# Wider first passes, context keys stacked on TensorE, and no idle matmuls in a two-attention decoder layer

## The chip, the cores and the metric

One core of one Trainium2 chip runs the whole program. The metric is the time on the device of one execution in microseconds (us). A core has five engines that run side by side and meet at semaphores: TensorE (PE in the profile, PEld for its weight loads), VectorE (DVE), ScalarE (ACT), GpSimd (POOL) and SyncE (SP), which here issues the DMA transfers.

## The reference

Two batches of 256 tokens with 128 features pass through three blocks, each followed by a residual sum and a layer norm. Block A is attention in which all 16 heads (8 features each) share one key and one value. Block X adds a causal self-attention (B below) and an attention over 512 context tokens (C below). The last block is a gated feed-forward over 8 experts, the best two weighted.

```python
q = (hidden_states @ Wq.T + bq) * SCALING        # block A: k and v are one head for all 16
scores = jnp.einsum('bthd,bsd->bhts', q, k)
probs = jax.nn.softmax(scores, axis=-1)
...
att = jnp.einsum('bhqd,bhkd->bhqk', q, k) * scale           # B, causal
y = jnp.einsum('bhqk,bhkd->bhqd', jax.nn.softmax(att, axis=-1), v)
attc = jnp.einsum('bhqd,bhkd->bhqk', qc, kc) * scale        # C, 512 context keys
y = y + jnp.einsum('bhqk,bhkd->bhqd', jax.nn.softmax(attc, axis=-1), vc)
...
for e in range(E):                                          # E = 8
    h = jnp.einsum('btd,hd->bth', x, W1[e]) + b1[e]
    a, b = jnp.split(h, 2, axis=-1)
    out = out + (jnp.einsum('bth,dh->btd', a * jax.nn.sigmoid(b), Wo) + bo) * comb[..., e:e + 1]
```

## The kernel before

Everything after the loads stays on the chip. Each engine works through its own list of jobs, written out by hand in the table `ORDER`. A token such as `SC0021:w0` is a job (kind SC, batch 0, query tile 0, pair 2, head 1 of the pair) and the PSUM buffer that it writes. An engine takes its jobs strictly in the order of the table, so a job that waits holds back all that stand behind it. A buffer is handed on by counters: `take` waits until its last reader has emptied it.

There are eight PSUM banks of 512 columns: three single buffers w0, w1 and w2, two double ones t0 and t1 (1024 columns), and y.

Scores are computed with bf16 operands at the accuracy of float32. A projection is split into three bf16 parts whose sum is the value (kinds h, d, f and g: ScalarE makes the high part, VectorE or GpSimd the two others), and the parts are stacked along the contraction rows, rows 0 to 47 for the even head of a pair of heads and 64 to 111 for the odd one, by matmuls with a matrix of zeros and ones (kinds R, line 380) and a copy (kinds e). The context keys are the exception: GpSimd makes their lower parts (`kc`, lines 1075 to 1080), and twelve DMAs (`K`, line 1181) put the parts in their rows.

Softmax takes two passes over the scores. The first (kinds S, lines 475, 491 to 494 and 502) computes them with queries on the partitions, and VectorE takes the largest of each row (kinds M, lines 796, 804 and 811), one buffer of 512 columns and one head at a time. The negated maxima are split into bf16 parts (kinds s), transposed by TensorE (kinds T, line 512) and copied (cT) to a row buffer; two DMAs for each group (kinds m, line 1171) write them into three more rows of the stacked queries. The second pass (kinds U, lines 522, 535 to 540 and 549) computes the transposed scores with the maximum already subtracted; ScalarE takes the exponential of 1024 columns (kinds E, line 979), and TensorE multiplies with the values (kinds P, lines 564, 582 and 599), where the row sum comes along as a ninth column. Kinds Y, n, Z, W, z, r, l and X transpose, normalise and project the result. Kinds F are the experts (lines 675 and 676).

The last digits of a job name batch, tile or group: UA10 is the second pass of block A, batch 1, pair 0. JQC0 (line 426) is the first projection of block X for batch 0. `N` (line 406) are matmuls on zeros whose result nobody reads.

## Time and profile before

| | us |
|---|---|
| median of 3 timed runs | 223.85 |
| lowest and highest | 222.95, 237.25 |
| the profiled execution, its own time | 221.34 |
| its span in the profile | 219.4 |

The span is what the trace covers, from the first to the last instruction. The execution's own time is 1.94 us longer. TensorE's clock as granted by the chip was 0.882 of full speed on average.

### The profile page before, as it was taken

How to read it: one execution, taken by the hardware profiler on the slowest of the kernel's cores; microseconds unless marked ns; L12 is line 12 of the kernel's file. 1: busy time of each engine (PE TensorE's matmuls, PEld its weight loads, DVE VectorE, ACT ScalarE, POOL GpSimd, SP SyncE). 2: the span in 40 equal slices, each digit the busy share in tenths (PEclk: the TensorE clock that was granted, in tenths of full speed). 3: DMA queues.
4: the chain of work that ended last, by engine and by line, in shares of the span. 5: the costliest groups of instructions: out<-in, count | busy, mean ns of one | idle time of the engine just before them, and what ended most of it. 6: DMA issues, size and time to landing. Idle time of an engine off the chain costs nothing.

```text
span 219.4 us, 4917 instructions
## 1 busy us (share of the span) xinstructions
PE 189.2 (86%) x1918; PEld 99.8 (45%) x1918; DVE 153.3 (70%) x390; ACT 103.0 (47%) x146; POOL 60.5 (28%) x171
## 2 busy tenths in 40 slices
PE   6979798840089999999989999999999999999981
PEld 3437243420024442455556545756576554445440
DVE  7983895850006857899789689793772589888883
ACT  3452075310057752446639866763957632242230
POOL 2199679431000010111440030020121316403204
PEclk9975558985559855899999999999999999999999
DMA  6960003555400000000000000000000000000001
GB/s 141 352 242 0 7 2 56 66 62 63 50 0 0 0 3 1 3 5 4 0 6 4 0 3 4 4 0 6 3 6 3 0 1 0 4 0 0 12 0 37
DMA packets 3910, 6.34 MB, mean 29 GB/s; under 512 B 880, under 2 KB 1640, under 8 KB 3888
## 3 DMA queue, kind: packets, MB, share of 16 engines
q1 hardware_dynamic: 3888, 6.03, 12.5%
q8 instruction: 15, 0.25, 0.5%
q14 instruction: 7, 0.06, 0.1%
HBM read 4.02 MB, written 0.26 MB: 20 GB/s over the span
## 4 chain that ended last, share of the span: by engine, by line
PE 67%; DVE 15%; DMA 9%; ACT 4%; issue 3%; POOLq 0%; POOL 0%; DVEq 0%; SPq 0%; ACTq 0%
PE t L675 9%; DMA q_stack_A<-mrow_A 8%; PE w L502 6%; PE y L599 6%; PE t L380 4%; PE t L549 4%; PE y L564 4%; PE w L491 3%; DVE mneg L811 3%; PE w L494 3%; PE w L475 3%; PE t L522 2%; PE t L676 2%; DVE mneg L796 2%; PE t L540 2%
## 5 line engine op out<-in xcount | busy, mean ns | idle before, releaser
L979 ACT ACTIVATE probs<-t 128x1024 f32<-128x1024 f32 x60 | 58.4, 1025 | 45.2 <-PE t L522 26.0
L811 DVE TENSOR_REDUCE mneg<-w 128x1 f32<-128x512 f32 x64 | 41.5, 685 | 7.3 <-PE w L502 6.8
L675 PE MATMUL t<-w1T,x1T 128*128 128x512 f32 x64 | 33.3, 601 | 0.2 <-DVE val_c L904 0.2
L796 DVE TENSOR_REDUCE mneg<-w 128x2 f32<-128x512 f32 x32 | 20.4, 686 | 4.9 <-PE w L475 4.5
L522 PE MATMUL t<-q_stack_A,k_stack_a 51*128 51x256 bf16 x64 | 9.4, 353 | 15.3 <-DMA q_stack_A<-mrow_A 14.5
L502 PE MATMUL w<-k_stack_c,q_stack_C 48*128 48x512 bf16 x64 | 21.7, 415 | 0.5
L1105 POOL CAST mpart<-mneg 128x8 bf16<-128x8 f32 (+1 forms) x11 | 2.1, 194 | 72.0 <-DVE mneg L811 48.9
L1018 ACT ACTIVATE part_c<-t 128x512 f32<-128x512 f32 x16 | 9.6, 597 | 26.1 <-PE t L676 24.0
L804 DVE TENSOR_REDUCE mneg<-w 128x2 f32<-128x512 f32 (+1 forms) x24 | 16.2, 686 | 7.7 <-PE w L494 7.6
L599 PE MATMUL y<-probs,v_c 128*32 128x128 f32 x512 | 17.2, 276 | 0.0
L475 PE MATMUL w<-k_stack_a,q_stack_A 48*128 48x256 bf16 x64 | 13.3, 344 | 2.7 <-DVE mneg L796 2.7
L675 PEld LDWEIGHTS t<-w1T,x1T 128*128 128x128 f32 x64 | 11.3, 190 | 8.3 <-issue 5.8
L599 PEld LDWEIGHTS y<-probs,v_c 128*32 128x32 f32 x512 | 13.0, 109 | 3.0 <-issue 1.9
L522 PEld LDWEIGHTS t<-q_stack_A,k_stack_a 51*128 51x128 bf16 x64 | 3.5, 108 | 20.7 <-DMA q_stack_A<-mrow_A 14.7
L549 PE MATMUL t<-q_stack_C,k_stack_c 51*128 51x128 bf16 x256 | 12.7, 218 | 0.2
L676 PE MATMUL t<-b_stack,bias_sel 128*128 128x512 bf16 x32 | 12.1, 379 | 0.0
L984 ACT ACTIVATE y_sb<-y 128x512 f32<-128x512 f32 x12 | 7.1, 595 | 10.3 <-PE y L564 5.3
L845 DVE COPY x1T<-w 128x256 f32<-128x256 f32 x2 | 0.8, 420 | 15.5 <-PE w L651 15.5
L920 DVE SCALAR_TENSOR_TENSOR ctx_room<-val_c,gate_comb,ctx_room 128x256 f32<-128x256 f32 x20 | 9.9, 494 | 1.7 <-DVE val_c L904 0.5
L549 PEld LDWEIGHTS t<-q_stack_C,k_stack_c 51*128 51x128 bf16 x256 | 7.7, 94 | 6.2 <-ACT probs L979 2.3
L564 PE MATMUL y<-probs,v_a 128*32 128x512 f32 x64 | 10.5, 749 | 0.0
L491 PE MATMUL w<-k_stack_b,q_stack_B 48*128 48x128 bf16 (+1 forms) x64 | 10.3, 270 | 0.0
(207 smaller groups left out, 316.6 us busy)
## 6 DMA issues: line engine op xcount, KB each, us to landing
w1T<-in_w1T SPq DMA_DIRECT2D x8, 256.0 KB, 6.7
k_stack_c<-part_c SPq DMA_DIRECT2D x12, 128.0 KB
rest<-in_rest SPq DMA_DIRECT2D x1, 772.0 KB, 7.5
bias_row<-in_rows SPq DMA_DIRECT2D x1, 384.0 KB, 6.1
ctx_room<-in_ctx SPq DMA_DIRECT2D x1, 320.0 KB, 5.3
first<-in_first SPq DMA_DIRECT2D x1, 262.5 KB, 2.8
q_stack_C<-mrow_C SPq DMA_DIRECT2D x16, 3.0 KB
out<-rest SPq DMA_DIRECT2D x4, 64.0 KB, 1.5
```

The costliest lines, as they stand in the source:

```text
L475: last = nc.tensor.matmul(o[:, a * T:(a + 1) * T], q_stack["A"][half(i), p, q0 + a * P:q0 + (a + 1) * P], k_stack_a[half(i), b, :], start= ...
L491: nc.tensor.matmul(o[:, m * keys:(m + 1) * keys], q_stack["B"][half(i), p, q0 + q * P:q0 + (q + 1) * P], k_stack_b[half(i), p, q0:q0 + key ...
L502: give(nc.tensor.matmul(o[:], q_stack["C"][half(i), p, q0 + q * P:q0 + (q + 1) * P], k_stack_c[half(i), p, b * TC:(b + 1) * TC], start=Tru ...
L522: last = nc.tensor.matmul(o[:, c0:c0 + T], k_stack_a[half(i, KROW), b, kt * P:(kt + 1) * P], q_stack["A"][half(i, KROW), p, q0:q0 + T], st ...
L549: last = nc.tensor.matmul(o[:, c0:c0 + P], k_stack_c[half(i, KROW), p, b * TC + kt * P:b * TC + (kt + 1) * P], q_stack["C"][half(i, KROW), ...
L564: last = nc.tensor.matmul(y_open[32 * j:32 * j + VW, :], v_a[:, 2 * b + kt, :], moving, start=(kt == 0), stop=(kt == 1), tile_position=(0, ...
L599: last = nc.tensor.matmul(y_open[32 * j:32 * j + VW, c * P:(c + 1) * P], v_c[:, 4 * b + kt, VD * head:VD * head + VW], probs[:, u, c0:c0 + P],
L675: nc.tensor.matmul(o, x2T[:, (2 * b + q) * P:(2 * b + q + 1) * P], w1T[:, e, :], start=True, stop=False)
L676: last = nc.tensor.matmul(o, bias_sel[:, e, :], b1_stack[:], start=False, stop=True)
L796: emptied(V.tensor_reduce(out=mneg[:, mb_of[("A", b, p // 4)], at:at + 9:8], in_=o[:].rearrange("p (a k) -> p a k", a=2), axis=AX.X, op=AL ...
L811: emptied(V.tensor_reduce(out=mneg[:, mb_of[("C", b, q, p // 4)], at:at + 1], in_=o[:], axis=AX.X, op=ALU.max, negate=True), src)
L979: emptied(A.activation(probs[:, n % NPT, :], o[:], ACT.Exp), src)
```

## The change

The PSUM banks are divided anew: one single buffer w0, three double ones t0, t1 and t2, and y.

A first-pass job now computes the scores of both heads of a pair into one double buffer, and one VectorE instruction reduces 1024 columns. Its matmuls alternate between the two halves of the contraction rows.

The lower bf16 parts of the queries and keys of block A and of the context keys are made on TensorE and ScalarE: a new job D repeats the projection and subtracts the parts that are already there by a matmul with the negated unit matrix, and ScalarE copies the remainder. For block X, VectorE subtracts, ScalarE makes the middle part and VectorE the last. The context keys are stacked like the others (RKC, eKC), so the twelve DMAs, GpSimd's parts and its eight fills of the key array go. The two R jobs of a projection run as one block of 24 matmuls over four groups of 32 rows. The factor of the scores moves into the exponential. All 12 idle matmuls go. The whole table `ORDER` is written anew; the diff shows a line of it.

```diff
--- before.py
+++ after.py
...
-        N3:w0 JQA0:w0 JQA1:w1 JKA0:w2 JKA1:w0 RQA00:t0 RQA01:t1 RKA0:w2 KC:t0 SA030:w1 SA031:w2 SA001:w0 SA011:w1 SA020:w0
...
+        JKA0:w0 VA:t0 JQA0:t1 DKA01 DQA01 DKA02 DQA02 RKA0:w0 JKA1:t2 RQA00:t1 JQA1:w0 RQA01:t0 DQA11 DKA11 SA02:t1 SA01:t0
...
-        w0 w1 w2 w3 w4 w5 w6 w7 mA00 mA01 K00 K10 K02 K12 K01 K11 K03 K13 K05 K15 K04 K14 bb mA10 mA11 mC000 mB00 mC001 mC010
-        mB01 mC011 mC100 mC101 mB10 mC110 mC111 mB11 st01 st10 st00 st11""",
+        w0 w1 w2 w3 w4 w5 w6 w7 mA00 bb mA01 mA10 mA11 mC001 mC000 mB00 mB01 mC010 mC011 mC100 mC101 mB10 mC110 mB11 mC111 st00
...
-        region = {"w0": ps("w0", [P, 512]), "w1": ps("w1", [P, 512]), "w2": ps("w2", [P, 512]),
-                  "t0": ps("t0", [P, 1024]), "t1": ps("t1", [P, 1024]), "y": ps("y", [P, 512])}
+        region = {"t0": ps("t0", [P, 1024]), "t1": ps("t1", [P, 1024]), "t2": ps("t2", [P, 1024]),
+                  "w0": ps("w0", [P, 512]), "y": ps("y", [P, 512])}
...
+                elif kind in ("DQA", "DKA", "DKC"):
+                    name, src, cols, count = split_of(kind, b)
+                    if once("ident_neg"):
+                        pe.wait_ge(s_ident_neg, 1)
+                    pe.wait_ge(s_parts[f"{name}{b}"], job[2])
+                    o = region[filled[src][0]][:, 0:count]
+                    if kind == "DKC":
+                        nc.tensor.matmul(o, wc[:, 0, :], ctxT[:, cols], start=True, stop=False)
+                    else:
+                        i = 0 if kind == "DQA" else 1
+                        nc.tensor.matmul(o, w_a[:, i * C:(i + 1) * C], x0T[b], start=True, stop=False)
+                    for r in range(job[2]):
+                        last = nc.tensor.matmul(o, ident_neg[:], parts_of[name][:, r, cols], start=False, stop=(r == job[2] - 1))
+                    last.then_inc(s_left[f"{name}{b}"], 1)
...
+                elif kind in ("RQA", "RQB", "RKB", "RQC", "RKC"):
+                    if once("sel"):
+                        pe.wait_ge(s_sel, 1)
+                    halves.append(take(slot, job))
+                    if job[2]:
+                        name = "qk"[kind[1] == "K"] + kind[2]
+                        side = 0 if kind[1] == "Q" else 1
+                        if kind[2] == "B" or kind == "RQC":
+                            pe.wait_ge(s_parts[f"{name}{b}"], 3)
+                        else:
+                            wait_emptied(pe, ("KC", b // 2) if kind == "RKC" else ("J" + kind[1:], b))
+                        values = parts_of[name][:, :, q0:q0 + T]
+                        lasts = {}
                         for j in range(2):
                             for r in range(3):
                                 for i in range(2):
-                                    c0 = i * 512 + j * T
-                                    last = select(o, slice(c0, c0 + T), side, j, r, 2 * job[2] + i, values[:, r, :])
-                    give(last, job)
+                                    for g in range(2):
+                                        c0 = i * 512 + j * T
+                                        lasts[g] = select(halves[g], slice(c0, c0 + T), side, j, r, 2 * g + i, values[:, r, :])
+                        for g in range(2):
+                            give(lasts[g], (kind, b, g))
+                        halves.clear()
...
                 elif kind == "SA":
-                    _, b, p, i = job
+                    _, b, p = job
                     if once(("kA", b)):
                         wait_emptied(pe, ("RKA", b))
                     if once(("qA", b, p // 4)):
                         wait_emptied(pe, ("RQA", b, p // 4))
                     o = take(slot, job)
                     for a in range(QT):
-                        last = nc.tensor.matmul(o[:, a * T:(a + 1) * T], q_stack["A"][half(i), p, q0 + a * P:q0 + (a + 1) * P],
-                                                k_stack_a[half(i), b, :], start=True, stop=True)
+                        for i in range(2):
+                            c0 = i * 512 + a * T
+                            last = nc.tensor.matmul(o[:, c0:c0 + T], q_stack["A"][half(i), p, q0 + a * P:q0 + (a + 1) * P],
+                                                    k_stack_a[half(i), b, :], start=True, stop=True)
...
                 elif kind == "SC":
-                    _, b, q, p, i = job
-                    if once("kC"):
-                        pe.wait_ge(s_kc, 16 * 12)
+                    _, b, q, p = job
+                    for n in (2 * b, 2 * b + 1):
+                        if once(("kC", n, p // 4)):
+                            wait_emptied(pe, ("RKC", n, p // 4))
                     if once(("qC", b, p // 4)):
                         wait_emptied(pe, ("RQC", b, p // 4))
                     o = take(slot, job)
-                    give(nc.tensor.matmul(o[:], q_stack["C"][half(i), p, q0 + q * P:q0 + (q + 1) * P],
-                                          k_stack_c[half(i), p, b * TC:(b + 1) * TC], start=True, stop=True), job)
+                    for i in range(2):
+                        last = nc.tensor.matmul(o[:, i * 512:(i + 1) * 512], q_stack["C"][half(i), p, q0 + q * P:q0 + (q + 1) * P],
+                                                k_stack_c[half(i), p, b * TC:(b + 1) * TC], start=True, stop=True)
+                    give(last, job)
...
                 elif kind == "MC":
-                    _, b, q, p, i = job
-                    src = ("SC",) + job[1:]
-                    at = 4 * i + p % 4
-                    o = wait_full(dve, src)
-                    emptied(V.tensor_reduce(out=mneg[:, mb_of[("C", b, q, p // 4)], at:at + 1], in_=o[:], axis=AX.X, op=ALU.max,
-                                            negate=True), src)
+                    _, b, q, p = job
+                    o = wait_full(dve, ("SC", b, q, p))
+                    dst = mneg[:, mb_of[("C", b, q, p // 4)], p % 4:p % 4 + 5:4]
+                    emptied(V.tensor_reduce(out=dst, in_=o[:].rearrange("p (i k) -> p i k", i=2), axis=AX.X, op=ALU.max,
+                                            negate=True), ("SC", b, q, p))
...
+                if kind in ("hQA", "hKA", "hQB", "hKB", "hQC", "hKC"):
+                    name, src, cols, count = split_of(kind, b)
+                    if name in left and job[2]:
+                        wait_emptied(act, src)
+                    else:
+                        o = wait_full(act, src)
+                        if job[2]:
+                            act.wait_ge(s_left[f"{name}{b}"], job[2])
+                    dst = parts_of[name][:, job[2], cols]
+                    value = left[name][:] if job[2] and name in left else o[:, 0:count]
                     if name in PROJ_BIAS:
-                        ins = A.activation(parts_of[name][:, 0, cols], o[:, 0:T], ACT.Identity,
-                                           bias=bias_col[:, PROJ_BIAS[name]:PROJ_BIAS[name] + 1], scale=PROJ_SCALE[name])
+                        ins = A.activation(dst, value, ACT.Identity, bias=bias_col[:, PROJ_BIAS[name]:PROJ_BIAS[name] + 1])
                     else:
-                        ins = A.activation(parts_of[name][:, 0, cols], o[:, 0:T], ACT.Copy)
-                    ins.then_inc(s_parts[f"{name}{b}"], 1)
-                elif kind in ("fQB", "fKB", "fQC"):
-                    name = "qk"[kind[1] == "K"] + kind[2]
-                    src = ("J" + kind[1:], b)
-                    o = wait_full(act, src)
-                    ins = A.activation(left[name][:, cols], o[:, 0:T], ACT.Identity,
-                                       bias=bias_col[:, PROJ_BIAS[name]:PROJ_BIAS[name] + 1], scale=PROJ_SCALE[name])
-                    if kind == "fQC":
-                        ins.then_inc(s_val[name], 1)
+                        ins = A.activation(dst, value, ACT.Copy)
+                    if job[2] < 2:
+                        ins.then_inc(s_parts[f"{name}{b}"], 1)
                     else:
                         emptied(ins, src)
...
-                    emptied(A.activation(probs[:, n % NPT, :], o[:], ACT.Exp), src)
+                    emptied(A.activation(probs[:, n % NPT, :], o[:], ACT.Exp, scale=SCALE), src)
...
-                elif kind == "kc":
-                    if b == 0:
-                        wait_emptied(pool, ("KC",))
-                    cols = slice(b * T, (b + 1) * T)
-                    link(G.tensor_tensor(val_c[:, cols], val_c[:, cols], part_c[:, 0, cols], ALU.subtract))
-                    link(G.tensor_copy(part_c[:, 1, cols], val_c[:, cols]))
-                    G.tensor_tensor(part_c[:, 2, cols], val_c[:, cols], part_c[:, 1, cols], ALU.subtract).then_inc(s_kc_parts, 1)
...
-                elif kind == "K":
-                    _, i, t = job
-                    if (i, t) == (0, 0):
-                        sp.wait_ge(s_ones_c, 1)
-                        sp.wait_ge(s_kc_high, 1)
-                    if (i, t) == (0, 1):
-                        sp.wait_ge(s_kc_parts, 4)
-                    row = HALF * i + D * t
-                    sp.dma_start(k_stack_c[row:row + D, :, :], part_c[half(i, HALF), TERM_PART_K[t], :]).then_inc(s_kc, 16)
...
```

How the change moves instructions, at three places. In these lists w and t stand for the PSUM buffers, `still` for the zeros.

SyncE's queue, from the first transfer of row maxima of block A on; before, and then after. `b_stack` is the stacked expert bias.

```order
L1171 DMA q_stack_A<-mrow_A 3x4x256 x4
L1181 DMA k_stack_c<-part_c 8x8x1024 x12
L1188 DMA b_stack<-gT 8x512 x2
L1188 DMA b_stack<-b_low 8x512
L1171 DMA q_stack_A<-mrow_A 3x4x256 x4
```

```order
L1155 DMA q_stack_A<-mrow_A 3x4x256 x2
L1163 DMA b_stack<-gT 8x512 x2
L1163 DMA b_stack<-b_low 8x512
L1155 DMA q_stack_A<-mrow_A 3x4x256 x6
L1155 DMA q_stack_C<-mrow_C 3x4x128 x4
```

The maxima of batch 1 stood behind the twelve key transfers and now follow those of batch 0 directly.

TensorE in block A, batch 0, up to the first transposed maxima (L512 before, L538 after) and the first second pass (L522, L548).

```order
L380 MATMUL w<-part_k,sel 128x256 x3
L464 MATMUL w<-ctx_room 128x128 x4
L416 MATMUL w<-first 128x8 x4
L475 MATMUL w<-k_stack_a,q_stack_A 128x256 x2
L512 MATMUL w<-ident_bf,mpart 24x128 x2
L475 MATMUL w<-k_stack_a,q_stack_A 128x256 x12
L522 MATMUL t<-q_stack_A,k_stack_a 128x256 x4
```

```order
L433 MATMUL w<-ctx_room 128x512
L438 MATMUL w<-part_c,ident_neg 128x512
L538 MATMUL t<-ident_bf,mpart 24x128 x2
L494 MATMUL t<-k_stack_a,q_stack_A 128x256 x4
L433 MATMUL w<-ctx_room 128x512
L438 MATMUL w<-part_c,ident_neg 128x512 x2
L373 MATMUL t<-part_q,sel 128x256 x24
L494 MATMUL t<-k_stack_a,q_stack_A 128x256 x4
L481 MATMUL w<-ctx_room 128x128 x4
L548 MATMUL t<-q_stack_A,k_stack_a 128x256 x8
```

The values (L416) and the context values (L464) leave the place ahead of the transposes; the remainders of the context keys (L433, L438), a stacking block and the context values now stand between the transposes and the second pass.

TensorE in block X: first passes over the context for batch 1 (L502, L527) among second passes (L549, L575) and value products (L599, L625) of batch 0.

```order
L502 MATMUL w<-k_stack_c,q_stack_C 128x512 x3
L599 MATMUL y<-probs,v_c 32x128 x16
L549 MATMUL t<-q_stack_C,k_stack_c 128x128 x8
L502 MATMUL w<-k_stack_c,q_stack_C 128x512 x2
L549 MATMUL t<-q_stack_C,k_stack_c 128x128 x8
```

```order
L527 MATMUL t<-k_stack_c,q_stack_C 128x512 x4
L575 MATMUL t<-q_stack_C,k_stack_c 128x128 x8
L625 MATMUL y<-probs,v_c 32x128 x16
L575 MATMUL t<-q_stack_C,k_stack_c 128x128 x8
L527 MATMUL t<-k_stack_c,q_stack_C 128x512 x4
```

First passes come in blocks of two pairs, in the same buffers as the second passes.

## Rows read from the trace of the kernel before

**Rows 1.** The page, part 1: busy us, share of the span, instructions.

```profile
span 219.4 us, 4917 instructions
PE 189.2 (86%) x1918; PEld 99.8 (45%) x1918; DVE 153.3 (70%) x390; ACT 103.0 (47%) x146; POOL 60.5 (28%) x171
```

**Rows 2.** The page, part 4: the chain that ended last, shares by engine.

```profile
PE 67%; DVE 15%; DMA 9%; ACT 4%; issue 3%; POOLq 0%; POOL 0%; DVEq 0%; SPq 0%; ACTq 0%
```

**Rows 3.** The chain in order of time, 43 to 66 us: start, us, what.

```profile
44.18 16.88 DMA q_stack_A<-mrow_A
...
65.65 0.45 PE w L426
```

**Rows 4.** The timeline, 22 to 62 us: start, us, engine, line, what.

```profile
22.98 1.62 SPq L1171 DMA_DIRECT2D q_stack_A<-mrow_A  x2
...
26.32 0.37 PE L522 MATMUL t<-q_stack_A,k_stack_a 51*128 51x256 bf16 x1
...
33.29 7.89 SPq L1181 DMA_DIRECT2D k_stack_c<-part_c  x12
...
43.37 5.14 SPq L1171 DMA_DIRECT2D q_stack_A<-mrow_A  x4
...
61.11 1.03 PE L522 MATMUL t<-q_stack_A,k_stack_a 51*128 51x256 bf16 x8 [14.48 <-DMA q_stack_A<-mrow_A]
```

**Rows 5.** Stretches: PE, PEld, DVE, ACT, POOL busy (instructions), PEclk, DMA, GB/s.

```profile
3.50:65.60 62.10, 42.28 (x263) 21.02 (x263) 34.08 (x91) 20.60 (x28) 29.45 (x76) 0.70 0.40 85
65.60:94.70 29.10, 28.81 (x223) 12.29 (x223) 21.67 (x40) 16.85 (x22) 1.86 (x10) 0.77 0.01 2
94.70:170.10 75.40, 73.05 (x1228) 44.58 (x1228) 56.97 (x129) 49.59 (x62) 14.01 (x42) 1.00 0.01 3
170.10:213.20 43.10, 42.28 (x200) 20.84 (x199) 35.27 (x102) 14.06 (x33) 11.45 (x28) 1.00 0.01 2
```

**Rows 6.** Stretches cut where the granted clock changes, same columns.

```profile
0.00:3.50 3.50, 1.46 (x3) 0.28 (x3) 2.50 (x21) 1.49 (x2) 1.38 (x10) 1.00 0.47 123
...
14.50:34.70 20.20, 18.72 (x101) 9.29 (x101) 13.50 (x26) 6.40 (x7) 16.55 (x49) 0.50 0.02 4
34.70:48.60 13.90, 9.94 (x83) 5.21 (x79) 10.16 (x27) 5.99 (x9) 7.38 (x19) 0.98 0.55 69
...
75.70:89.10 13.40, 13.36 (x70) 4.59 (x66) 9.09 (x15) 4.60 (x6) 0.79 (x4) 0.50 0.01 2
```

**Rows 7.** The timeline of TensorE, 131 to 135 us, at full clock.

```profile
131.85 1.38 PE L380 MATMUL t<-part_k,sel 32*128 32x256 bf16 x24
...
134.57 0.40 PE L549 MATMUL t<-q_stack_C,k_stack_c 51*128 51x128 bf16 x8
134.81 0.59 PE L502 MATMUL w<-k_stack_c,q_stack_C 48*128 48x512 bf16 x2
135.33 1.08 PE L599 MATMUL y<-probs,v_c 128*32 128x128 f32 x32
```

**Rows 8.** The timeline of TensorE among the experts, at full clock.

```profile
192.94 1.02 PE L675 MATMUL t<-w1T,x1T 128*128 128x512 f32 x2
193.80 0.38 PE L676 MATMUL t<-b_stack,bias_sel 128*128 128x512 bf16 x1
194.01 0.27 PE L657 MATMUL w<-ident,x 128*128 128x128 f32 x1
```

**Rows 9.** The timeline of VectorE and ScalarE: reductions in a row, copies of 1024 columns.

```profile
131.67 3.20 DVE L811 TENSOR_REDUCE mneg<-w 128x1 f32<-128x512 f32 x5 [0.19 <-PE w L502]
...
138.24 1.27 DVE L790 TENSOR_SCALAR k_stack_b<-t,row_ones 128x1024 bf16<-128x1024 f32 x1
...
132.72 1.11 ACT L966 ACTIVATE k_stack_b<-t,row_ones 128x1024 bf16<-128x1024 f32 x1 [0.38 <-PE t L380]
```

**Rows 10.** The timeline around the first group of maxima, 17 to 22 us.

```profile
17.51 0.66 POOL L1078 TENSOR_TENSOR val_c<-val_c,part_c 128x256 f32<-128x256 f32 x1
...
19.33 0.20 POOL L1105 CAST mpart<-mneg 128x16 bf16<-128x16 f32 x1
```

More of the change, by code:

```diff
@@ L25 @@
 NEG = -1.0e30
-ONES = 1.0019378662109375
 HALF = 64
@@ new lines @@
+        RKC01:t1 YA00:w0 YA01:t2 UA10:t0 ZA0:w0 UA11:t2 UA12:t1 WA0:w0 UA13:t0 SA15:t2 RKC20:t1 RKC21:t2 XA0:w0 PA100 TA11:t0
+        JQC0:w0 JKB0:t1 JQB0:t0 PA101 JV0:w0 RQC00:t0 RQC01:t1 UA14:t2 SC005:t1 UA15:t0 SC001:t2 SC006:t1 SC003:t0 UA16:t2
+        UA17:t0 SC004:t2 SC007:t1 RQB00:t0 PA110 RQB01:t2 PA111 SC002:t1 SC000:t2 TC001:w0 YA11:w0 RKB00:t1 RKB01:t0 SC011:t2
+        YA10:w0 SB001:t0 TC000:t2 SB000:t1 ZA1:w0 SB011:t2 SB012:t0 SB013:t1 WA1:w0 SB010:t2 UC000:t1 UC001:t2 UC002:t1 TB00:w0
@@ L327, in stacked @@
                 return k_stack_a[:, b, :]
-            dst = k_stack_b if job[0] == "RKB" else q_stack[job[0][2]]
+            dst = {"RKB": k_stack_b, "RKC": k_stack_c}.get(job[0], q_stack[job[0][2]])
             return dst[:, 4 * job[2]:4 * job[2] + 4, b * T:(b + 1) * T]
@@ L431, in _ @@
-                    give(last, job)
-                elif kind in ("RQA", "RKA", "RQB", "RKB", "RQC"):
+                            last = nc.tensor.matmul(o[:, i * C:(i + 1) * C], x1T[:, q0 + i * P:q0 + (i + 1) * P], wx[:, 3, :],
+                                                    start=True, stop=True)
+                    else:
+                        i = ("JQB", "JKB", "JQC").index(kind)
+                        last = nc.tensor.matmul(o[:, 0:T], wx[:, i, :], x1T[:, q0:q0 + T], start=True, stop=True)
@@ L453, in _ @@
                     o = take(slot, job)
-                    for i in range(2):
-                        last = nc.tensor.matmul(o[:, i * 512:(i + 1) * 512], wc[:, 0, :],
-                                                ctxT[:, i * 512:(i + 1) * 512], start=True, stop=True)
-                    give(last, job)
+                    give(nc.tensor.matmul(o[:, 0:TC], wc[:, 0, :], ctxT[:, b * TC:(b + 1) * TC], start=True, stop=True), job)
                 elif kind == "VC":
```

262 lines of the change are left out of this document (106 added, 156 removed).

## The prediction

> **What bounds the kernel now.** I read the page first: TensorE is busy for 189.2 of 219.4 us, VectorE for 153.3 and ScalarE for 103.0 [rows 1], and the chain that ended last lies on TensorE for 67%, on VectorE for 15% and on DMA for 9% [rows 2]. So TensorE's work counts first, and one transfer stands out. The chain in order of time shows it: 16.88 us from 44.18 us on for two rows of maxima of a few KB, and the first projection of block X (JQC0) starts only at 65.65 us [rows 3]. The timeline tells why. The same kind of transfer for batch 0 is issued at 22.98 us, and the second pass that needs it starts at 26.32 us, 3.3 us later. For batch 1 the issue is at 43.37 us and the start at 61.11 us. Between the two stand the twelve key transfers, issued from 33.29 us on [rows 4], and the DMA engines are 0.55 busy from 34.7 to 48.6 us [rows 6].
>
> I cut the span at JQC0, and at 94.7, 170.1 and 213.2 us [rows 5]. Stretch one (3.5 to 65.6 us) has TensorE busy for 42.3 of 62.1 us at a mean clock of 0.70. In the other three it is busy for 144.1 of 147.6 us, VectorE for 113.9 (77%), ScalarE for 80.5. What is cheaper on TensorE there should show, as long as VectorE can follow. After 213.2 us come 6.2 us of closing steps that the change leaves alone, but for idle matmuls beside them.
>
> **Prices at full clock.** Of TensorE I take the distance from start to start, since a record's length holds a tail. Two records of a float32 matmul of 512 columns take 0.86 us and a bf16 one of 512 columns 0.21 us [rows 8]; with half the columns I take half, 0.43 and 0.11 (estimates). Eight second-pass matmuls of 128 columns take 0.24 us [rows 7], although in a row they would need 0.43 at the bf16 price: neighbours in opposite halves of the rows run together. Two first-pass matmuls of 512 columns plus what lies between take 0.52 us before the value product starts [rows 7]; 0.43 of it is their columns. 24 stacking matmuls over two row groups take 1.38 us [rows 7], about 1.3 without the tail.
>
> **The change part by part.**
>
> *The key transfers go.* Batch 1's maxima then need about 3.3 us from issue to use as batch 0's did: start at 46.7 instead of 61.1 us, **-14.4**. Next late is TensorE's own order: XA0 and JQC0 stand behind UA10 to UA13 and came 4.5 us after UA10 (65.65 against 61.11). JQC0 at 51.3 us, if nothing else in stretch one changed.
>
> *Work that TensorE gains in stretch one*, at full clock: remainders D for block A, 4 x (0.43+0.11) + 4 x (0.43+0.21) = 4.7; for the context keys, 2 x (0.86+0.21) + 2 x (0.86+0.43) = 4.7; four stacking blocks RKC between 0.7 (four row groups at once, half of 1.3) and 1.3, near the middle as weight loads bind, 4 x 1.0 = 4.0; PA100 moves ahead of JQC0, 1.0. It loses 8 idle matmuls (1.7) and, since both heads run together, 16 x (0.43 - 0.27) = 2.6. Net **+10.1 at full clock**. The clock sets the price: before it was at its lower level, 1.2 GHz, from 14.5 to 34.7 us, and at 2.4 GHz around that [rows 6]. D, float32 over all rows, is denser than what stood there; I take a mean of 0.85, so 11.9 us, with ends 10.1 and 20.2. Beside it lies the idle time of TensorE outside the DMA wait, 62.1 - 42.3 - 14.5 = 5.3 us. Also gone is a wait on GpSimd, whose key parts (from 17.51 us) held the first split of maxima back to 19.33 us: 1.8 [rows 10]; the split is on VectorE now. Stretch one: 51.3 + 11.9 - 5.3 - 1.8 = **56.1 us**. If all additions hid, 49.5; with the low clock throughout, 64.4.
>
> The D jobs put two round trips between TensorE and ScalarE ahead of the first scores, in place of VectorE's steps. No row shows such a trip; it lies between nothing (queries and keys alternate, so each hides the other's) and some 1 us each, a D of 0.54 to 0.64 and half of a copy that takes 1.11 for four times the columns [rows 9]. I take nothing, as TensorE is the busier one; the 2 us stay in the range.
>
> *ScalarE and VectorE in stretch one.* Evictions of stacked keys: 5 x 1.11 on ScalarE and 3 x 1.27 on VectorE [rows 9]; six key parts of 512 columns, at half the copy's price some 0.6 each (an estimate). ScalarE is busy for 20.6 of 62.1 us there [rows 5], so it covers them. VectorE loses the lower parts of block A and gets 16 reductions instead of 32.
>
> *First passes from JQC0 on.* 64 context matmuls in 32 pairs: 32 x (0.43 - 0.24) = 6.1. Causal ones: four pairs of tile 0 and eight of tile 1 save 0.21 each, 2.5. Six pairs of stacking blocks, 1.3 to 1.0 each: 1.8. Four idle matmuls 0.9, and PA100's 1.0. Together **-12.3**. Five reductions in a row take 3.20 us, so 0.63 each start to start [rows 9]; 512 columns at VectorE's pace are nearly all of it, so a double one should take 1.15 to 1.25, the price of the copy of 1024 columns (1.27) being an upper bound. 44 of them instead of 88 save VectorE 0 to 5 us, and two more evictions take 2.5. VectorE's 113.9 us stay within 3 us. In 135 us that is 84%, so it will bind more often, with all double buffers shared: I give **+2** back, between 0 and 12.3. These stretches: 147.6 - 12.3 + 2 = **137.3 us**, 130 to 148.
>
> **The sum.** 56.1 + 137.3 + 6.2 = 199.6 us of span, plus the 1.9 around it: **201.5 us**, I say 201, against the profiled execution's 221.34. The timed median was 2.5 above that; the other runs scatter by more, and I add nothing. About 2% is what a measurement of this kernel can tell from no change.
>
> **A rule on the clock.** The trace shows the clock at 2.4 GHz from the start, even before the first idle matmul at 1.2 us [rows 6], and at 1.2 GHz from 14.5 us on. The Trainium skill, page "TensorE: Matmul & The Clock Gate", Part 1, says that the throttled state is the default and that activity releases it; by it the start without idle matmuls would be slow. The first rows disagree with that default here. By the rule the first 3 us of work on TensorE would take 6, 204 us in all; by the rows nothing is added. It speaks for rival one and leaves the sum alone.
>
> **The rivals.**
>
> *One, the clock stays low in stretch one.* For it: from 14.5 to 34.7 us TensorE is busy for 18.7 of 20.2 us and still at 1.2 GHz [rows 6], so being busy does not raise it, and three of the idle matmuls stood at the very start. Against: from 94.7 us on, where float32 products recur all the time, it stays at 2.4 GHz [rows 5], and D is float32. Price: 20.2 instead of 11.9, so JQC0 at 64.4 us; **210 us**. Chance 0.16.
>
> *Two, the readers bind after JQC0.* S and U share three double buffers. Each holds one for its fill, 1.0 to 1.2 us of reading and two hand-overs, some 1.75 us; 100 such uses (44 first passes, 44 second, 12 stackings) are 175 us over three buffers, 58 us of some 100. That speaks against it on average, VectorE's 84% for it. All 12.3 us come back: **212 us**. Chance 0.14. The Trainium skill, page "TensorEngine Tiling (Array Packing)", PSUM Bottleneck, says that tiling speeds up TensorE but not the emptying of PSUM, which is this rival; by it the sum loses the 12.3.
>
> *Three, the change does not do what it says:* the transfer of maxima was late for another reason than the queue behind the keys. The DMA share of 0.55 while the keys' transfers are under way speaks against it [rows 6]. JQC0 would come 14.4 later, **216 us**. Chance 0.03.
>
> *Four, slower.* w0 is now the only small buffer; 45 jobs after JQC0 use it (projections, transposes), where three stood. TensorE's order is strict, so a job that waits for w0 stops all scores behind it. A hand-over is about 0.8 us by estimate, a fill of 0.2 and half of a 1024-column copy; most w0 jobs have others between them. It decides from 0.5 us of stop per use: 22.4 / 45. At 0.65 the time is **231 us**. Chance 0.03.
>
> *Five, better:* all additions of stretch one hide, and VectorE's 5 us count as well: 49.5 + 130.3 + 6.2 + 1.9, **188 us**. Chance 0.07.
>
> **How the numbers follow.** The forecast itself, 190 to 208, has 0.57. The range 187 to 214 holds it, rivals one and two and half of five. Faster by over 2% (below 219.4) has 0.95, within 2% 0.03, slower 0.02.
>
> **What would show it.** UA10 within 4 us of its transfer's issue and no PE wait on DMA over 3 us; JQC0 at 50 to 62 us; the clock in 5 to 50 us above 0.7; reductions of 1024 columns near 1.2 us; two context first-pass matmuls 0.24 us apart from the next work; VectorE 80 to 86% busy from JQC0 to the end. The prediction is wrong if TensorE shows waits on w0 or t buffers of over 10 us in all, or if stretch one ends after 65 us.

## The result, and the profile after

The changed kernel takes **205.2 us** (four runs, 203.09 to 207.77) where the kernel before takes 223.85 (the median of its compared runs, 222.95 to 225.05). The ratio is **0.913, 95% interval 0.902 to 0.924**. The profiled execution took 207.77 us, for a span of 206.0. Some executions of a program run longer at a lower granted clock (the mean clock of TensorE over the span); they are left out of every ratio and of what is called a compared run, and the one profiled here, at 0.914 against 0.936 and 0.937 of the others, is one of them.

The page of after, part 1 (busy us, share, instructions) and the chain that ended last, by engine:

```profile
PE 180.4 (88%) x2044; PEld 97.3 (47%) x2044; DVE 148.1 (72%) x326; ACT 115.8 (56%) x171; POOL 44.0 (21%) x136
...
PE 72%; DVE 13%; ACT 9%; issue 3%; DMA 1%; POOLq 0%; POOL 0%; DVEq 0%; ACTq 0%
```

Against [rows 1] TensorE is busy 9 us less, ScalarE 13 more, and DMA, 9% of the chain in [rows 2], has fallen to 1%. The stretches to JQC0 and from there to the 6.2 us of closing steps, as in [rows 5] (PE, PEld, DVE, ACT, POOL busy; granted clock; DMA share; GB/s), of after:

```profile
3.50:57.66 54.16, 48.12 (x405) 24.78 (x405) 33.60 (x73) 31.98 (x45) 17.10 (x48) 0.91 0.22 69
57.66:199.80 142.14, 130.92 (x1635) 71.62 (x1634) 109.18 (x225) 81.92 (x123) 22.80 (x70) 0.93 0.01 3
```

and of before, the last three stretches of [rows 5] taken as one:

```profile
65.65:213.20 147.55, 144.14 (x1645) 77.68 (x1646) 113.91 (x270) 80.45 (x116) 27.33 (x79) 0.95 0.01 3
```

JQC0 comes 8.0 us earlier, and what follows is 5.4 us shorter. In the second stretch TensorE is busy 13.2 us less, but idle for 11.2 us instead of 3.4. The wait for the maxima is gone. [Rows 4] shows it before; this is the same place in the timeline of after, SyncE's issue first and TensorE below:

```profile
45.19 1.44 SPq L1155 DMA_DIRECT2D q_stack_A<-mrow_A  x2
...
49.13 0.39 PE L548 MATMUL t<-q_stack_A,k_stack_a 51*128 51x256 bf16 x4 [0.28 <-ACT k_stack_c L975]
```

UA10 starts 3.9 us after the issue and waits 0.28 us for the buffer that ScalarE still reads (`k_stack_c`, line 975), not for DMA. The start of the program is new too:

```profile
7.19 1.06 PE L436 MATMUL w<-first 128*128 128x256 f32 x2
8.04 0.42 PE L438 MATMUL w<-part_k,ident_neg 128*128 128x256 bf16 x1
...
10.29 0.60 PE L436 MATMUL t<-first 128*128 128x256 f32 x2
10.72 0.38 PE L438 MATMUL t<-part_q,ident_neg 128*128 128x256 bf16 x2
```

Two float32 records of the same shape take 0.85 us from start to start at 7.19 us and 0.43 us at 10.29, though the clock column reads 1.00 for both. So the work of the first microseconds runs at half speed, and the column does not show it. The trace of the kernel before has the same slow start behind its three idle matmuls:

```profile
3.54 3.82 PE L411 MATMUL w<-first 128*128 128x256 f32 x8 [0.87 <-DMA first<-in_first]
```

The next job starts at 7.29 us, so these eight float32 records take 3.75 us, 0.94 for two where 0.43 is full speed. The first scores start at 14.95 us in after (10.27 before). The costliest groups (busy us, mean ns, idle before, releaser) of after:

```profile
L984 ACT ACTIVATE probs<-t 128x1024 f32<-128x1024 f32 x60 | 58.9, 1025 | 18.3 <-PE t L575 14.5
L821 DVE TENSOR_REDUCE mneg<-t 128x2 f32<-128x1024 f32 x32 | 37.7, 1218 | 9.2 <-PE t L527 9.1
...
L808 DVE TENSOR_REDUCE mneg<-t 128x4 f32<-128x1024 f32 x16 | 18.8, 1216 | 8.5 <-PE t L494 8.4
```

### The profile page after: what moved, and what is told of

The parts are those of the page before. It is cut to its first block, busy times and chain, and to the rows that moved or that the text cites. A ratio compares the mean times of both kernels' runs of the same rounds, so it can differ in the third digit from the quotient of the medians.

```text
span 206.0 us, 5104 instructions
## 1 busy us (share of the span) xinstructions
PE 180.4 (88%) x2044; PEld 97.3 (47%) x2044; DVE 148.1 (72%) x326; ACT 115.8 (56%) x171; POOL 44.0 (21%) x136
## 4 chain that ended last, share of the span: by engine, by line
PE 72%; DVE 13%; ACT 9%; issue 3%; DMA 1%; POOLq 0%; POOL 0%; DVEq 0%; ACTq 0%
PE t L701 14%; PE y L625 9%; ACT probs L984 5%; PE t L373 5%; PE t L575 4%; PE y L590 4%; DVE mneg L821 3%; PE t L702 3%; PE t L527 3%; DVE mneg L808 3%; PE y L608 3%; DVE mneg L815 2%; PE t L566 2%; PE t L561 2%; PE w L433 2%
## 5 line engine op out<-in xcount | busy, mean ns | idle before, releaser
L984 ACT ACTIVATE probs<-t 128x1024 f32<-128x1024 f32 x60 | 58.9, 1025 | 18.3 <-PE t L575 14.5
L821 DVE TENSOR_REDUCE mneg<-t 128x2 f32<-128x1024 f32 x32 | 37.7, 1218 | 9.2 <-PE t L527 9.1
L808 DVE TENSOR_REDUCE mneg<-t 128x4 f32<-128x1024 f32 x16 | 18.8, 1216 | 8.5 <-PE t L494 8.4
L625 PE MATMUL y<-probs,v_c 128*32 128x128 f32 x512 | 19.1, 294 | 0.0
L527 PE MATMUL t<-k_stack_c,q_stack_C 48*128 48x512 bf16 x64 | 13.4, 455 | 2.6 <-ACT q_stack_C L977 1.0
L625 PEld LDWEIGHTS y<-probs,v_c 128*32 128x32 f32 x512 | 14.2, 117 | 3.0 <-issue 1.4
L575 PE MATMUL t<-q_stack_C,k_stack_c 51*128 51x128 bf16 x256 | 12.5, 229 | 3.4 <-DVE mneg L815 1.1
L815 DVE TENSOR_REDUCE mneg<-t 128x4 f32<-128x1024 f32 (+1 forms) x12 | 14.0, 1215 | 1.7 <-PE t L516 1.7
L701 PEld LDWEIGHTS t<-w1T,x1T 128*128 128x128 f32 x64 | 11.2, 191 | 8.0 <-issue 5.9
L575 PEld LDWEIGHTS t<-q_stack_C,k_stack_c 51*128 51x128 bf16 x256 | 8.1, 99 | 10.3 <-issue 4.9
L930 DVE SCALAR_TENSOR_TENSOR ctx_room<-gated,gate_comb,ctx_room 128x256 f32<-128x256 f32 x18 | 8.8, 489 | 1.0
L914 DVE SCALAR_TENSOR_TENSOR gated<-part_c,t 128x512 f32<-128x512 f32 x11 | 7.5, 684 | 2.3 <-ACT part_c L1023 1.9
L963 ACT ACTIVATE part_c<-w,first 128x512 bf16<-128x512 f32 x6 | 4.1, 687 | 7.9 <-PE w L438 6.3
L494 PE MATMUL t<-k_stack_a,q_stack_A 48*128 48x256 bf16 x64 | 6.9, 289 | 1.4 <-DVE mneg L808 0.8
L548 PE MATMUL t<-q_stack_A,k_stack_a 51*128 51x256 bf16 x64 | 7.0, 294 | 1.0 <-DVE mneg L821 0.6
L527 PEld LDWEIGHTS t<-k_stack_c,q_stack_C 48*128 48x128 bf16 x64 | 3.1, 97 | 9.4 <-issue 3.5
```

What stands on the lines that cost most here:

```text
L527: last = nc.tensor.matmul(o[:, i * 512:(i + 1) * 512], q_stack["C"][half(i), p, q0 + q * P:q0 + (q + 1) * P], k_stack_c[half(i), p, b * TC ...
L575: last = nc.tensor.matmul(o[:, c0:c0 + P], k_stack_c[half(i, KROW), p, b * TC + kt * P:b * TC + (kt + 1) * P], q_stack["C"][half(i, KROW), ...
L625: last = nc.tensor.matmul(y_open[32 * j:32 * j + VW, c * P:(c + 1) * P], v_c[:, 4 * b + kt, VD * head:VD * head + VW], probs[:, u, c0:c0 + P],
L701: nc.tensor.matmul(o, x2T[:, (2 * b + q) * P:(2 * b + q + 1) * P], w1T[:, e, :], start=True, stop=False)
L808: emptied(V.tensor_reduce(out=dst, in_=o[:].rearrange("p (i a k) -> p i a k", i=2, a=2), axis=AX.X, op=ALU.max, negate=True), ("SA", b, p))
L815: emptied(V.tensor_reduce(out=dst, in_=o[:].rearrange("p (i m k) -> p i m k", i=2, m=count), axis=AX.X, op=ALU.max, negate=True), ("SB", b ...
```

## The experiments

### The maxima ahead of the keys

In the kernel before, SyncE's order alone:

```diff
-w7 mA00 mA01 K00 K10 ... K04 K14 bb mA10 mA11 mC000
+w7 mA00 mA01 mA10 mA11 K00 K10 ... K04 K14 bb mC000
```

> The kernel before, with only SyncE's order changed: the two transfers of batch 1's maxima stand ahead of the twelve key transfers and the bias transfers. Theory (the maxima were late because they stood behind the keys in one queue): UA10 starts within 4 us of its transfer's issue, at about 47 us instead of 61.1, JQC0 at about 51. The keys are now issued from about 44 us on and, at the 15 us that they took before from first issue to the end of the traffic, land at about 59 us, so the first context scores may wait for them some 4 us. Time 207 to 214 us, ratio 0.93 to 0.955. Rival (they were late for another reason): UA10 stays after 57 us, ratio within 2% of 1.

Its two compared runs took 227.8 and 227.9 us, before 223.8 in the same sitting and 222.7 to 223.7 in the next: no gain, 4 us lost. Timeline of SyncE, then of TensorE, in this run:

```profile
42.85 5.69 SPq L1171 DMA_DIRECT2D q_stack_A<-mrow_A  x4
48.66 7.94 SPq L1181 DMA_DIRECT2D k_stack_c<-part_c  x12
...
46.59 0.61 PE L522 MATMUL t<-q_stack_A,k_stack_a 51*128 51x256 bf16 x8
...
50.74 0.93 PE L426 MATMUL w<-x1T,rest 128*128 128x256 f32 x2 [0.28 <-DVE x1T L845]
...
75.56 0.60 PE L502 MATMUL w<-k_stack_c,q_stack_C 48*128 48x512 bf16 x1 [17.39 <-DMA k_stack_c<-part_c]
```

The first half of the theory holds: UA10 at 46.59 us, JQC0 at 50.74, as worked out. The second half had the keys wrong: from first issue to use they need 27 us, not 15. Issued at 33.29 us as before, they are there at about 60, just when the maxima behind them are. The page of the kernel before shows it, beyond the 48.6 us to which I had read the DMA share in [rows 6]: in its row of GB/s each number is a slice of 5.5 us, and the traffic lasts from slice seven, at 32.9 us, to the end of slice eleven, at 60.3:

```profile
GB/s 141 352 242 0 7 2 56 66 62 63 50 0 0 0 3 1 3 5 4 0 6 4 0 3 4 4 0 6 3 6 3 0 1 0 4 0 0 12 0 37
```

So two transfers were late together in the kernel before, and putting one wholly ahead only shows the other. An order in between was not run: six keys ahead of the maxima and six behind. At 27 us for twelve, an estimate puts the first six through at about 47 us and the rest at about 61, and in this run TensorE came to its first context scores at 58.2 us (75.56 less 17.39).

### The keys on another queue

ScalarE issues the twelve key transfers; SyncE keeps the maxima:

```diff
 act: ... EA04 EA05
+K00 K10 K02 K12 K01 K11 K03 K13 K05 K15 K04 K14
 EA06 EA07 yA01 ...
```

> The kernel before, with the twelve key transfers issued by ScalarE, after the sixth exponential, instead of by SyncE; the maxima stay where they are. Theory (the queue alone made them wait): UA10 within 5 us of its transfer's issue, JQC0 at 51 to 58 us, since ScalarE gives up to 8 us for twelve issues at the 0.66 us that SyncE takes for one; ratio 0.94 to 0.98. Rival (the keys' traffic on the shared DMA engines makes the wait, whatever the queue): the maxima still land some 15 us after the issue and the ratio is within 2% of 1.

One compared run, 222.1 us, too few for a ratio. The profiled run (granted clock 0.805) shows where the transfers went; ScalarE's queue, SyncE's, TensorE:

```profile
35.75 1.17 ACTq L975 DMA_DIRECT2D k_stack_c<-part_c  x1
...
36.95 7.17 ACTq L975 DMA_DIRECT2D k_stack_c<-part_c  x11
...
51.07 1.54 SPq L1178 DMA_DIRECT2D q_stack_A<-mrow_A  x2
...
62.92 1.03 PE L522 MATMUL t<-q_stack_A,k_stack_a 51*128 51x256 bf16 x8 [7.84 <-DMA q_stack_A<-mrow_A]
```

The rival holds: with nothing ahead of them in their own queue, the maxima are still used 11.9 us after their issue, 27 us after the first key went out (35.75 us). It is the keys' traffic that they wait for, not the queue. Why they wait while the DMA engines are about 0.55 busy no view shows: the share is a mean over 16 engines, and does not tell whether those that carry the keys are full.

### No keys at all

```diff
-K00 K10 K02 K12 K01 K11 K03 K13 K05 K15 K04 K14 bb
+bb
-                        pe.wait_ge(s_kc, 16 * 12)
+                        pe.wait_ge(s_ones_c, 1)
```

> The kernel before without its twelve key transfers: it leaves out the stacking of the context keys, which stay constant ones (same matmuls, same shapes). In the run with the maxima first, UA10 started at 46.6 us and JQC0 at 50.7, but the keys then landed 27 us after their first issue and TensorE waited 17.4 us for them. Theory (keys and maxima both wait for the same traffic, and only its removal frees the 14.4 us): JQC0 at 51 us, no PE wait on DMA over 3 us, time 209 to 210 us, ratio 0.935 (0.93 to 0.94). Rival (part of the freed time is given back later, because the work after JQC0 then meets the lower clock or full buffers): JQC0 at 51 us too, but ratio 0.945 to 0.97.

Ratio **0.916 (0.908 to 0.923)**; its compared runs took 203.9 and 205.0 us. That is more than either theory gave: 19 us, **as much as the whole change**. The profiled run was slower (212.6 us at 0.879) and shows the wait gone: the maxima are issued at 46.14 us and used at 50.34, and no wait on DMA is over 1.0 us. Its JQC0 comes at 54.48 us, not 51, with a clock of 0.70 from 3.5 us to there. The 14.5 us of waiting are the larger part of the 19. The rest goes with the clock. In the profiled run of before 20.7 us ahead of the wait (43.1 x 0.24 x 2) and 19.0 us behind it were at the lower level; the whole span of these two runs had 27.5 and 31.3 us (span times one minus the mean, times two, with 0.932 and 0.923). About 10 us less at half speed are up to 5 us less work. Why the clock stays up longer there no run here shows.

### Block A's remainders on VectorE

The D jobs of block A are left out of TensorE's order, and VectorE gets `dKA01 dQA01 dKA02 dQA02 eKA0 vA dQA11 dKA11 dQA12 dKA12`, the form that block B keeps.

> The changed kernel, with block A's remainders formed by VectorE from one subtraction and one more, as in the kernel before, instead of by the eight D jobs on TensorE. The trace of after has the first reduction at 15.4 us against 11.5 before. Theory (the D round trips cost the start some 4 us, which I had booked at nothing): first reduction at 11.5 to 13 us and the end 3 to 4.5 us earlier, ratio to before 0.895 to 0.90 where after has 0.913. Rival (what is late at the start is covered by the transfer of maxima and by ScalarE's queue before JQC0): first reduction earlier, JQC0 and the end within 1 us of after, ratio 0.91 to 0.915.

Compared runs 208.8, 209.3 and 209.5 us: **4 us slower than after**, where both theories had it faster or equal. TensorE's and VectorE's timelines:

```profile
14.27 0.61 PE L494 MATMUL t<-k_stack_a,q_stack_A 48*128 48x256 bf16 x4 [1.21 <-ACT q_stack_A L979]
...
22.70 1.91 PE L433 MATMUL w<-ctx_room 64*128 64x512 f32 x2
...
15.87 0.67 DVE L774 TENSOR_TENSOR part_k<-left_kA,part_k 128x256 bf16<-128x256 f32 x1
16.47 4.61 DVE L810 TENSOR_REDUCE mneg<-t 128x4 f32<-128x1024 f32 x4
```

Two things go against it. VectorE's order puts batch 1's remainders ahead of the first reduction, 16.47 us instead of 15.38. And TensorE was at half speed for far longer: four score matmuls take 0.61 us (0.39 in after), and the float32 pair at 22.70 us still takes 1.91 us (1.02 in after at 20.28). It ends only near 46 us, between two equal sets of value products:

```profile
43.91 1.93 PE L590 MATMUL y<-probs,v_a 128*32 128x512 f32 x8
...
46.10 1.06 PE L590 MATMUL y<-probs,v_a 128*32 128x512 f32 x8
```

The clock column reads 1.00 all the while, and JQC0 came at 62.8 us. TensorE is busy for 50.0 us up to there, with the eight D jobs gone (48.1 in after with them). That its order had more waits at the start may be why the clock came late; no run shows it. So this run does not tell what D costs or saves at equal clock.

### Idle matmuls at the start, three and six

```diff
-JKA0:w0 VA:t0 JQA0:t1
+N3:w0 JKA0:w0 VA:t0 JQA0:t1      (N6:w0 in the second kernel)
```

> The changed kernel, with the three idle matmuls (six records) back at the start of TensorE's order, ahead of JKA0. In after the granted clock reads 1.00 from the start, but the pairs of D records of 4.6 to 9.5 us stand 0.85 us apart where later ones of the same shape stand 0.43 apart. Theory (TensorE starts at half speed and only work brings it up): the D pairs at 0.43 us from the first on, first reduction 1.5 to 2.5 us earlier, ratio to before 0.900 to 0.908. Rival (the slow start is something else, or is hidden): first reduction within 0.5 us, ratio 0.911 to 0.915.

> The changed kernel, with six idle matmuls ahead of JKA0 instead of none, so that TensorE works without a break from 1.2 us until the first load has come (3.6 us) and beyond. With three of them there was a break of 0.9 us, and the float32 records were at half speed until 11.9 us, as long as or longer than in after (9.7 us). Theory (an unbroken start brings full speed sooner): records of 256 float32 columns 0.60 us long in pairs from about 6 us on, first reduction 1.5 to 2.5 us earlier than 15.4 and the time 1 to 2 us lower. Rival (idle matmuls do not do what the D jobs do): full speed not before 9.5 us, first reduction at 15.4 to 16.5 us, time as after.

Three: compared runs 202.8, 203.0 and 204.2 us, beside 203.1, 205.1 and 205.3 of after: the same within the scatter, with full speed only from 11.9 us on. Six: ratio **0.905 (0.887 to 0.923)**, 203.3 to 205.8 us in its three compared runs, the same again. But in its trace the start is the one that the theory drew:

```profile
1.20 2.74 PE L399 MATMUL w<-still 128*128 128x512 bf16 x6 [1.20 <-DVE still L742]
...
5.56 0.59 PE L436 MATMUL w<-first 128*128 128x256 f32 x2
...
12.46 0.39 PE L494 MATMUL t<-k_stack_a,q_stack_A 48*128 48x256 bf16 x4
```

Full speed from about 4.2 us, and the first scores 2.5 us earlier. In this trace the gain reached JQC0, at 55.42 us instead of 57.66, although later stretches at half speed were longer (a clock of 0.87 to JQC0, 0.91 in after). In the times it is not clear of the scatter. Nor do six idle matmuls see to the start: in the run below with the same six, the D pairs were 0.85 us apart until 10.2 us.

### The context keys' remainders on VectorE

```diff
 pe:  ... -DKC01 -DKC02 -DKC11 -DKC12
 act: ... -hKC02 -hKC12
 dve: ... sA00 +dKC01 MA04 MA06 +dKC02 ... MA16 +dKC11 MA10 MA17 +dKC12 MA13 MA14 sA10
```

> The changed kernel, with the remainders of the context keys (four D jobs of 512 columns on TensorE) formed by VectorE instead, from a subtraction and one more; ScalarE copies the middle part only. Block A keeps its D jobs. TensorE loses 4.7 us at full clock (my term), VectorE gains 4 x 0.7 = 2.8 us. Theory (TensorE, busy for 48.1 of 54.2 us, sets stretch one): JQC0 at 52 to 55 us instead of 57.7 and the time 3 to 5 us lower. Rival (as where block A's remainders went to VectorE: TensorE is busier with D, comes to full speed sooner for it, and VectorE's reductions are pushed back): JQC0 within 1.5 us of 57.7 and the time within 2 us of after, or longer.

> Both edits together: context keys' remainders on VectorE, six idle matmuls at the start. If both theories hold: 4 to 7 us under after, 198 to 201 us. If neither does: 203 to 207 us, as after.

Ratios **0.915 (0.902 to 0.929)** and **0.909 (0.896 to 0.922)**, compared runs 205.5 to 207.8 and 204.3 to 206.7 us (the first edit alone, then both). By its marks the rival holds: JQC0 at 57.56 us, as in after, and no time under those of after. The first stretch of the first edit:

```profile
3.50:57.56 54.06, 44.68 (x390) 24.80 (x391) 34.40 (x77) 30.85 (x43) 17.54 (x48) 0.84 0.20 69
```

TensorE is busy for 3.4 us less than in after and idle for 3.4 us more (9.4 against 6.0), at a clock of 0.84 instead of 0.91. So the work taken off did not show. But it is not shown that the edit was the reason for the lower clock, as the clock of one unchanged program scatters more than this (the last experiment). There JQC0 comes at 57.66 us at 0.91 and at 61.58 at 0.78, which by a straight line gives 59.8 at 0.84, an estimate: at equal clock some 2 us of the 4.7 may have been gained.

### The heads one after the other

```diff
-q_stack["C"][half(i), p, ...], k_stack_c[half(i), p, ...]
+q_stack["C"][half(0), p, ...], k_stack_c[half(0), p, ...]
```

> The changed kernel, with both matmuls of each context first pass reading rows 0 to 47 (it leaves out the scores of the odd heads there and computes the even ones twice), so that no two neighbours lie in opposite halves of the rows. My term for running both heads together was 32 x 0.19 = 6.1 us. Theory (TensorE binds from JQC0 on): each pair takes 0.43 instead of 0.24 us start to start and the time rises by 4 to 6 us over after (205.2), ratio 0.932 to 0.942. Rival two (the readers bind): the pairs lengthen but the time rises by less than 2 us, ratio under 0.922.

The one compared run took 208.6 us at a clock of 0.933, 3.4 more than after (205.2 at 0.936): short of the 4 to 6 of the theory and above the rival's 2. The profiled one took 213.0 at 0.918 (after 207.8 at 0.914). Its four context matmuls at 140.78 us come 0.22 us apart, where after has four of them in 0.44. Its second stretch:

```profile
57.28:205.00 147.72, 137.82 (x1627) 74.12 (x1634) 109.39 (x224) 81.88 (x123) 22.75 (x70) 0.92 0.01 3
```

5.6 us longer than after's 142.14, for 6.1 us that I had booked. Up to 1.8 of it is the clock, by an estimate: at 0.92 and 0.93 the stretches had 23.6 and 19.9 us at half speed. So from JQC0 on, what TensorE works shows for the most part, 3.8 to 5.6 of 6.1 us, but not in full.

### Half the reductions' columns, half the exponentials'

```diff
-in_=o[:].rearrange("p (i k) -> p i k", i=2), axis=AX.X
+in_=o[:].rearrange("p (i k) -> p i k", i=2)[:, :, 0:256], axis=AX.X
```

and likewise the context exponentials over `[:, :, 0:256]` in the other kernel.

> The changed kernel, with the 32 context reductions reading 2 x 256 instead of 2 x 512 columns (it leaves out half of the keys in the maxima). VectorE loses 32 x 0.6 = 19 us. Rival two (VectorE binds after JQC0): the time falls by 5 to 10 us, ratio 0.87 to 0.89. If TensorE binds nearly everywhere: by less than 2 us, ratio over 0.904.

> The changed kernel, with the 32 context exponentials over 2 x 256 instead of 2 x 512 columns (it leaves out half of the keys in the weights). ScalarE loses 32 x 0.43 = 13.7 us. If ScalarE's reading of the double buffers holds TensorE back after JQC0: 3 to 7 us less, ratio 0.88 to 0.90. If TensorE or VectorE binds: less than 2 us, ratio over 0.904.

Half the reductions: 199.2 us in its one compared run, at 0.963. Others took 203.7 at 0.938, and 206.3 and 206.5 at 0.914, where after had 203.1 to 205.3 at 0.937 and 207.8 at 0.914: at most some 1.5 us less at the same clock. Half the exponentials: ratio **0.893 (0.887 to 0.898)**, 198.7 to 199.7 us, at 0.96. The second stretches, of half the reductions and of half the exponentials:

```profile
52.89:191.30 138.41, 127.52 (x1627) 70.67 (x1634) 93.67 (x225) 81.85 (x123) 22.85 (x70) 0.95 0.01 3
```

```profile
54.25:190.70 136.45, 125.91 (x1627) 69.73 (x1634) 109.79 (x225) 68.69 (x123) 22.74 (x70) 0.96 0.01 3
```

By its time the second fits "ScalarE holds TensorE back". The rows say otherwise. TensorE's idle time is 10.9 and 10.5 us, against 11.2 in after: taking 16 us off VectorE or 13 off ScalarE hardly shortens it. What shrinks is TensorE's busy time, by 3.4 and 5.0 us, and most of that is the clock: at 0.93, 0.95 and 0.96 the stretches had 19.9, 13.8 and 10.9 us at half speed, worth some 3.0 and 4.5 (estimates, from a clock of two digits). The run with the context keys' remainders on VectorE has the unchanged order from JQC0 on, and at 0.95 its stretch took 139.9 us: beside it half the reductions are worth 1.5. Waits of TensorE in 50 to 200 us tell why the idle time stays (us in all, times, longest); after, then half the reductions, then half the exponentials:

```profile
PE t L575 <- DVE mneg L815: 1.1, 2, 0.6
PE t L575 <- ACT probs L984: 1.1, 2, 0.8
PE t L575 <- DVE mneg L821: 1.1, 2, 0.6
...
PE t L527 <- ACT probs L984: 0.7, 2, 0.5
```

```profile
PE t L575 <- ACT probs L984: 1.8, 2, 1.0
...
PE t L575 <- DVE mneg L815: 1.1, 2, 0.6
PE t L527 <- ACT probs L984: 1.1, 4, 0.5
```

```profile
PE t L527 <- DVE mneg L821: 1.3, 3, 0.5
...
PE t L575 <- DVE mneg L815: 1.1, 2, 0.6
PE t L575 <- DVE mneg L821: 1.1, 2, 0.6
```

Make one reader faster and TensorE waits more for the other: for ScalarE's exponentials at lines 527 and 575 2.9 us instead of 1.8, for VectorE's reductions at line 527 1.3 instead of 0.8. Both read the same three double buffers in a fixed order, and each fill waits for whoever holds the next. A run with both readers made faster at once, which would show whether the idle time then goes, was not made.

### The changed kernel again

> The changed kernel once more, unedited, to have its scatter and its trace beside the other runs on the same chip. Expected: the runs between 203 and 208 us, as before, ratio 0.905 to 0.925, and at equal granted clock the same times within 1 us.

Six runs: 202.0 us at a granted clock of 0.951, and five of 210.2 to 211.8 at 0.89 to 0.90, longer than I had expected. With the first four (203.1 at 0.937, 205.1 and 205.3 at 0.936, 207.8 at 0.914) the ten lie near one line, some 9 us for 0.06 of mean clock, though not within the 1 us that I had expected (203.1 and 205.3 at the same clock). Five profiled runs have the same program up to JQC0:

| run | JQC0, us | clock, 3.5 us to JQC0 | TensorE busy |
|---|---|---|---|
| half the reductions | 52.89 | 1.00 | 44.4 |
| half the exponentials | 54.25 | 0.97 | 45.0 |
| heads one after the other | 57.28 | 0.91 | 47.5 |
| after | 57.66 | 0.91 | 48.1 |
| again | 61.58 | 0.78 | 53.0 |

The two ends, as the view gives them:

```profile
3.50:52.89 49.39, 44.39 (x403) 23.33 (x405) 31.02 (x73) 31.79 (x45) 17.14 (x48) 1.00 0.23 76
```

```profile
3.50:61.58 58.08, 53.02 (x402) 27.17 (x404) 33.08 (x73) 32.11 (x45) 17.09 (x48) 0.78 0.21 64
```

Same instructions, 8.7 us apart, and TensorE's busy time differs by 8.6: the difference goes with the time at half speed. The column misses the start here too: with half the reductions the float32 pairs stay 0.85 us apart until 11.9 us, in this run only until 9.1. I found no version that beats the changed kernel by more than the scatter. At equal clock a gain may hide in it: at 0.897 the changed kernel took 211.0 us here, with the context keys' remainders on VectorE 207.6 to 209.9, and with six idle matmuls besides 206.4 to 207.9.

## Why the prediction was right, and where its steps were off

- **The key transfers, -14.4: the time came, for a reason only half seen.** JQC0 at 50.74 us with the maxima first (51.3 worked out). But I took the maxima to be late because they stood behind the keys in a queue. The keys were as late themselves, 27 us from first issue to use, and the maxima wait for that traffic on either of two queues. Of what was tried only the removal pays. It paid 19 us, not 14.4.
- **Stretch one at 56.1 us: right in the total** (57.66, and 52.9 to 61.6 by the clock), and that is in part luck. The sum added 11.9 us of work and took back all 5.3 us in which TensorE idled. In after TensorE is busy for 5.8 us more (48.12 against 42.28), as the stretch also ran at 0.91 where before had 0.70, and it still idles for 6.0. Two terms were off by about 6 us each and cancel. At full clock the same sum gives 51.3 + 10.1 - 5.3 - 1.8 = 54.3; the run with a column of 1.00 had 52.9, with 5.0 us idle. Rival one is no other case than the forecast but the upper end of its scatter: 61.6 us at 0.78, where I had 64.4 throughout at the lower level.
- **D round trips at nothing: too low.** First scores at 14.95 us instead of 10.27. With full speed from 4.2 us they start at 12.46: 2.2 us are D and its trips, as my upper end said, 2.5 the slow start. How much of it reaches JQC0 is open: with six idle matmuls JQC0 came 2.2 us earlier, but in the run with half the reductions the first scores stood at 15.96 us and JQC0 at 52.89.
- **"The first rows disagree with that default here": wrong.** I read the clock column, which is 1.00 from the start. The records are at half speed until nearly 10 us in after (the pair at 9.32 us takes 0.75), and until 7 us in the trace of before that I had. The Trainium skill, page "TensorE: Matmul & The Clock Gate", Part 1, has the throttled state as the default, released by activity; by that rule the trace agrees. The 3 us that I priced it at came from no row; on the first scores it measured 2.5.
- **First passes, -12.3: right in size.** TensorE is busy 13.2 us less from JQC0 on, though at 0.93 instead of 0.95; undoing the pairing alone gives back 3.4 us in the compared run and up to 5.6 in the trace, of 6.1.
- **"+2 give-back": the term that was mis-sized.** TensorE's idle time there grew by 7.8 us (3.4 to 11.2), 6.4 of it at fills of double buffers that a reader still held (thirteen waits at lines 527, 548, 561 and 575, none over 0.8 us; under the 10 us that I had named as the sign of being wrong). This is rival two in part. I argued from VectorE's share, which is 77%, not the 84% worked out; the waits pass between two readers of three buffers, and no one reader's load measures them. The Trainium skill, page "TensorEngine Tiling (Array Packing)", PSUM Bottleneck, says that tiling speeds up TensorE but not the emptying of PSUM. With that the trace agrees in part: 6.4 us of waits for buffers still held, against 13.2 us less of busy time, and not the 12.3 that the rival gave back.
- **Smaller prices.** Reductions of 1024 columns 1.22 us (1.15 to 1.25 given). Two context first-pass matmuls 0.22 us apart (0.24): four of them in 0.44 us at 136.27. A stacking of both halves at once, four row groups, 0.77 us (1.0 given, 0.7 to 1.3), so weight loads did not hold it up as I had argued. w0, now the only small buffer, cost next to nothing: rival four is out. Rival three is out.
- **The sum.** 57.66 + 142.14 + 6.2 = 206.0 us of span against 199.6: +1.6 in stretch one, +4.8 after it, in an execution that was 2.6 us above the median. The rest of the change, all that is not the keys' transfers, nets to nothing: 203.9 and 205.0 us without them and without any of it, 203.1 to 205.3 with it. I had it at -5.5 (11.9 - 5.3 - 1.8 - 12.3 + 2). The keys paid some 4.5 us more than forecast and the rest some 5.5 less: that 201.5 lies so near 205.2 is in part luck.

## What to carry to other kernels

When a small transfer is late behind large ones, ask when the large ones are needed, too, and read from the page how long their traffic lasts: moving the small one ahead here turned a wait of 14.5 us into one of 17.4. TensorE work that is "free" because the engine idles must be priced at both clock levels, and the range of a time made of it is as wide as the clock's own scatter. Where two engines empty a rotation of buffers, the price of faster fills is read from TensorE's waits for either, not from the busy share of one.
